# A three-deep store ring and W2 read in place by TensorE, in the expert stage of a graph-attention plus mixture-of-experts layer

## What is computed

```
x = x + elu(softmax(mask(leaky_relu(e), adj)) @ (layernorm(x) @ W))     # graph attention
n = layernorm(x)
idx = argmax(n @ router_w.T + router_b)                                 # one of 32 experts a token
h = relu(n @ W1[idx] + b1[idx])                                         # 256 -> 64
x = x + relu(h @ W2[idx] + b2[idx])                                     # 64 -> 256
```

## Time and profile before

| | |
|---|---|
| median of 3 runs | 1364.01 us (1361.14 to 1366.87) |
| the profiled execution's own time | 1360.98 us |
| its span (first to last instruction) | 1359.4 us |
| DVE busy over the span | 1064.8 us (78%) |
| PE / ACT / POOL busy | 827.6 / 729.6 / 619.2 us |
| the expert stage: first to last `yb` written | 1187.4 to 1346.6 us |

### The profile page before, as it was taken

How to read it: one execution, slowest core, us unless ns; L and a number is a source line. 1 busy time by engine, 2 the same in 40 slices (tenths; PEclk the granted TensorE clock), 3 DMA queues, 4 the chain that set the end, 5 groups by cost and what they waited for, 6 DMA issues and landing times.

```text
span 1359.4 us, 24132 instructions
## 1 busy us (share of the span) xinstructions
PE 827.6 (61%) x3116; PEld 631.0 (46%) x3116; DVE 1064.8 (78%) x4589; ACT 729.6 (54%) x1359; POOL 619.2 (46%) x651
## 2 busy tenths in 40 slices
PE   3766636666656656666665666566666775276663
PEld 2444435445444445445454454454544663154442
DVE  5888848888888888899988888889988764355553
ACT  3666846556666556665566655566654110155553
POOL 2111145544555445554455554545545772245553
PEclk9888956666666666666666666666666666589998
DMA  7999988887888887888888888878883246444442
GB/s 260 330 344 342 344 305 312 336 323 302 309 330 323 324 327 299 308 327 334 335 314 312 329 324 324 325 298 326 337 333 112 78 99 125 156 121 120 126 123 63
DMA packets 110969, 365.64 MB, mean 269 GB/s; under 512 B 28840, under 2 KB 62081, under 8 KB 78163
## 3 DMA queue, kind: packets, MB, share of 16 engines
q1 hardware_dynamic: 80610, 302.25, 59.5%
q0 software_dynamic: 28288, 61.66, 13.8%
q10 hardware_dynamic: 2034, 1.37, 0.3%
HBM read 352.05 MB, written 32.05 MB: 283 GB/s over the span
## 4 chain that ended last, share of the span: by engine, by line
DVE 40%; issue 28%; PE 12%; DMA 10%; DVEq 3%; POOL 3%; ACT 2%; POOLq 1%; ACTq 0%; SPq 0%
DVE top_word L854 7%; DMA out_x<-yb,tok 7%; DVE top_pos L860 4%; PE psL L1510 4%; DVE diag L1059 3%; PE psW L1431 2%; PE psT L1501 2%; PE psL L1511 2%; POOL G_all L590 2%; DVE xn L1103 2%; DVE st L909 1%; DVE el L1076 1%; DMA G_all<-wh_table,idx 1%; DVE begun L1002 1%; DVE code L868 1%
## 5 line engine op out<-in xcount | busy, mean ns | idle before, releaser
L590 POOL DMA_INDIRECT G_all<-wh_table,idx x384 | 399.0, 1039 | 231.5 <-issue 103.9
L699 ACT ACTIVATE sg<-raw_all,minus_half 128x2048 fp8e4<-128x2048 int32 x256 | 504.2, 1992 | 0.0
L1491 PE MATMUL psO<-G_all,diag 128*128 128x256 f32 x640 | 281.3, 623 | 91.8 <-DVE diag L1059 91.8
L1491 PEld LDWEIGHTS psO<-G_all,diag 128*128 128x128 f32 x640 | 200.7, 326 | 141.3 <-issue 96.4
L724 ACT ACTIVATE xT<-psT 128x256 f32<-128x256 f32 x64 | 24.5, 383 | 390.4 <-PE psT L1501 390.4
L854 DVE MAX8 top_word<-sg 128x8 f32<-128x512 f32 x256 | 174.4, 681 | 2.8 <-issue 0.4
L860 DVE FIND_INDEX8 top_pos<-top_word,sg 128x8 uint32<-128x512 f32 x256 | 175.3, 685 | 0.6 <-issue 0.6
L612 POOL DMA_INDIRECT regions<-x,posu x64 | 67.8, 1059 | 149.1 <-DVE posu L1141 145.9
L653 POOL DMA_INDIRECT out_x<-yb,tok x81 | 82.1, 1013 | 90.2 <-DVE yb L1376 72.0
L1431 PE MATMUL psW<-w_aug,xT 128*128 128x258 f32 x256 | 80.9, 445 | 8.0 <-ACT xT L691 7.6
L606 POOL TENSOR_TENSOR x<-ve,minus_half 128x1 f32<-128x1 f32 x64 | 36.0, 563 | 101.7 <-DVE x L1099 101.5
(11 more groups left out here) (209 smaller groups left out, 1882.9 us busy)
## 6 DMA issues: line engine op xcount, KB each, us to landing
raw_all<-in_adj SPq DMA_DIRECT2D x256, 1024.0 KB, 6.5
xb<-regions SPq DMA_DIRECT2D x84, 130.0 KB, 2.1
wh_table<-G_all POOLq DMA_DIRECT2D x8, 1040.0 KB, 11.0
w_sb<-in_x SPq DMA_DIRECT2D x8, 1024.0 KB, 8.2
xr<-in_x SPq DMA_DIRECT2D x64, 128.0 KB, 4.9
G_all<-wh_table,idx POOLq DMA_INDIRECT x384
w_sb<-in_L_ffn_W SPq DMA_DIRECT2D x2, 1024.0 KB
w_sb<-in_L_ffn_W SPq DMA_DIRECT2D x4, 512.0 KB
```

The lines of the kernel that those rows point to most:

```text
L590: pool.indirect_dma_start(out=G[par][:, k, :], out_offset=None, in_=table[:, :], in_offset=bass.IndirectOffsetOnAxis(ap=idx[par][:, k:k + ...
L699: act.activation(sg[par][q][:, :], raw[q], ACT.Sign, bias=minus_half[:, 0:1], saturate=False).then_inc(a_sg, 1)
L1491: pe.matmul(psO[par][:, 0:D], diag[:, k, :], G[par][:, k, 0:D], start=(k == 0), stop=False)
```

## The change

It has four parts in the expert stage and one at the start of the program.

- `yb`, `tok` and `y_out` come three times and not twice.
- DVE's `copy_w2` and the tiles `w2_b` are gone. PE's `block_output` reads the expert's number into a register and reads `w2_sb` in place at that offset. It has a wait on `v_y` (the rows of block b - 2 are written), which protects `psO`.
- b1 becomes a column of `w1_sb` behind the 128 columns of W1's two halves, 129 columns an expert. ACT makes one copy and not two. PE reads the stationary operand of half h at columns h*64 to h*64+128 of the copy.
- W1 is loaded by eight DMAs of half the size in place of four, b1 by one DMA that now stands behind the wait for the first stage's rows, and PE waits for the weights' arrival; DVE does not any more.
- Since the matmul reads 128 rows of `w2_sb`, rows 64 to 127 are set to zero by a DVE memset of 64 x 8192 elements among the program's first instructions. A plan instruction of DVE falls away.

```diff
+STORES = 3
-        w1_sb = sb("w1_sb", [P, E, DH, H])
-        b1_t = sb("b1_t", [H, E])
-        w2_sb = sb("w2_sb", [H + 1, E, D])
+        w1_sb = sb("w1_sb", [P, E, DH * H + 1])
+        w2_sb = sb("w2_sb", [P, E, D])
-        w1_b = [sb(f"w1_b{i}", [P, DH, P]) for i in range(2)]
-        b1_b = [sb(f"b1_b{i}", [H, 1]) for i in range(2)]
-        w2_b = [sb(f"w2_b{i}", [P, D]) for i in range(2)]
+        w1_b = [sb(f"w1_b{i}", [P, H + P]) for i in range(2)]
-        yb = [sb(f"yb{i}", [P, D]) for i in range(2)]
-        tok = [sb(f"tok{i}", [P, 1], u32) for i in range(2)]
+        yb = [sb(f"yb{i}", [P, D]) for i in range(STORES)]
+        tok = [sb(f"tok{i}", [P, 1], u32) for i in range(STORES)]
...
-                act.activation(b1_b[r % 2][:, :], b1_t[:, bass.ds(e, 1)], ACT.Copy)
-                act.activation(w1_b[r % 2][:, :, 0:H],
-                               w1_sb[:, bass.ds(e, 1), :, :].rearrange("p o h n -> p (o h) n"), ACT.Copy).then_inc(a_w1, 1)
+                act.activation(w1_b[r % 2][:, 0:DH * H + 1], w1_sb[:, bass.ds(e, 1), :].rearrange("p o n -> p (o n)"),
+                               ACT.Copy).then_inc(a_w1, 1)
...
-                v.memset(w1_b[par][:, :, :], 0.0)
-                v.memset(w2_b[par][:, :], 0.0)
+                v.memset(w1_b[par][:, :], 0.0)
+            v.memset(w1_sb[:, E - 1, DH * H:DH * H + 1], 0.0)
+            v.memset(w2_sb[H:P, :, :], 0.0).then_inc(w2_zero, 1)
             v.memset(slot_s[:, :], 0.0).then_inc(v_const, 1)
...
-                if not isinstance(b, int) or b > 1:
-                    v.wait_ge(y_out[r % 2], (b - r % 2) * 8)
+                if not isinstance(b, int) or b >= STORES:
+                    v.wait_ge(y_out[r % STORES], turn * 32 + r // STORES * 16)
...
-            blocks_loop(v, [(copy_w2, 2), (block_norm, 0), (block_rows, 3)])
+            blocks_loop(v, [(block_norm, 0), (block_rows, 3)])
...
+                e = pe.value_load(plan_i[0:1, bass.ds(b + P, 1)], min_val=0, max_val=E - 1)
                 pe.wait_ge(a_hT, b + 1)
-                pe.matmul(psO[r % 2][:, 0:D], hT[r % 2][:, :], w2_b[r % 2][:, :],
+                pe.wait_ge(v_y, b + RING - 1)
+                pe.nop(nofuse=True)
+                pe.matmul(psO[r % 2][:, 0:D], hT[r % 2][:, :], w2_sb[:, bass.ds(e, 1), :].rearrange("p o n -> p (o n)"),
                           start=True, stop=True).then_inc(pe_y, 1)
+            pe.wait_ge(ffn_in, 16 * 12)
```

More of the change, by code:

```diff
@@ L290, in gat_moe @@
         a_xb = sem("a_xb")
[L291 removed]
+        w2_zero = sem("w2_zero")
         a_w1 = sem("a_w1")
@@ L296, in gat_moe @@
         v_y = sem("v_y")
-        y_out = [sem(f"y_out{i}") for i in range(2)]
+        y_out = [sem(f"y_out{i}") for i in range(STORES)]
         VP = 8
@@ L653, in store_block @@
                 pool.indirect_dma_start(
[L654 to L656 removed]
+                    out=out[:, :], out_offset=bass.IndirectOffsetOnAxis(ap=tok[r % STORES][:, 0:1], axis=0),
+                    in_=yb[r % STORES][:, :], in_offset=None, bounds_check=last_row, oob_is_err=False
+                ).then_inc(y_out[r % STORES], 16)
             steps = blocks_loop(pool, [(store_block, TAIL)])
             with pool.If(steps > TURNS * RING):
[L660 to L663 removed]
+                for k in range(STORES):
+                    pool.wait_ge(y_out[k], 16 * ((BLOCKS + STORES - 1 - k) // STORES))
+                    pool.nop(nofuse=True)
             with pool.If(steps < TURNS * RING + 1):
[L665 to L667 removed]
+                rows_out = pool.value_load(steps_i[0:1, 1:2], min_val=16, max_val=16 * BLOCKS)
+                for k in range(STORES):
+                    pool.wait_ge(y_out[k], rows_out)
                     pool.nop(nofuse=True)
@@ L805, in hidden @@
                 act.wait_ge(a_w1, b + 1)
[L806 to L807 removed]
+                act.activation(hT[r % 2][0:H, :], psH[r % 2][0:H, 0:P], ACT.Relu,
+                               bias=w1_b[r % 2][0:H, DH * H:DH * H + 1]).then_inc(a_hT, 1)
+            act.wait_ge(ffn_in, 16 * 12)
             act.wait_ge(v_plan, PLAN_STEPS)
@@ L1372, in block_rows @@
                 v.wait_ge(pe_y, b + 1)
-                if not isinstance(b, int) or b > 1:
-                    v.wait_ge(y_out[r % 2], (b - r % 2) * 8)
-                v.tensor_copy(tok[r % 2][:, :], xb[r][:, D + 2:D + 3])
-                v.scalar_tensor_tensor(out=yb[r % 2][:, :], in0=psO[r % 2][:, 0:D], scalar=0.0, in1=xb[r][:, 0:D],
+                if not isinstance(b, int) or b >= STORES:
+                    v.wait_ge(y_out[r % STORES], turn * 32 + r // STORES * 16)
+                v.tensor_copy(tok[r % STORES][:, :], xb[r][:, D + 2:D + 3])
+                v.scalar_tensor_tensor(out=yb[r % STORES][:, :], in0=psO[r % 2][:, 0:D], scalar=0.0, in1=xb[r][:, 0:D],
                                        op0=ALU.max, op1=ALU.add).then_inc(v_y, 1)
-            def copy_w2(b, r, turn):
-                e = v.value_load(plan_i[0:1, bass.ds(b + P, 1)], min_val=0, max_val=E - 1)
-                v.tensor_copy(w2_b[r % 2][0:H + 1, :], w2_sb[:, bass.ds(e, 1), :].rearrange("p o n -> p (o n)")).then_inc(v_w2, 1)
-            v.wait_ge(ffn_in, 16 * 8)
-            blocks_loop(v, [(copy_w2, 2), (block_norm, 0), (block_rows, 3)])
+            blocks_loop(v, [(block_norm, 0), (block_rows, 3)])
         @block.tensor
@@ L1581, in block_hidden @@
                 for h in range(DH):
-                    mm = pe.matmul(psH[r % 2][:, 0:P], w1_b[r % 2][:, h, :], xTb[r % 2][:, h, :],
+                    mm = pe.matmul(psH[r % 2][:, 0:P], w1_b[r % 2][:, h * H:h * H + P], xTb[r % 2][:, h, :],
                                    start=(h == 0), stop=(h == DH - 1))
```

40 lines of the change are left out of this document (14 added, 26 removed).

## The result

| | changed | before, beside it |
|---|---|---|
| median | 1354.68 us (1348.75 to 1356.49, 6 runs) | 1363.87 us (1360.32 to 1366.87, 6 runs) |
| ratio | 0.9929 [0.9904, 0.9953] | |
| profiled execution: own time, span | 1356.24, 1354.6 us | 1360.98, 1359.4 us |
| first to last `yb` | 144.8 us, 1.81 a block | 159.2 us, 1.99 a block |

The kernel is 9.2 us faster; forecast were 31. The time lies outside the range of 1320 to 1350 us.

What follows compares the result with a forecast made beforehand. The two-buffer ring of stores was taken to bound the kernel at 1.99 us a block. The stage's -33.2 us and the start's +2.1 gave -31.1, so 1364.0 became 1333 us, range 1320 to 1350.

Steps and rivals of the forecast that it cites:

- The loads: Expert stage, refilling `xb`: landing plus some 0.35 us around it, 1.2 to 1.5 us a block, nearly always below other floors.
- The bulk: Expert stage after its first six blocks: 74 blocks at 1.54 us, from floors of 1.31 to 1.44 plus 0.1 for unevenness.
- the loop between DVE and PE: Expert stage: norm, transposes, `psO` and rows close a loop of two steps, 2.88 us, 1.44 a step, the highest floor.
- The six slow blocks: Start of the expert stage: at the 1.2 GHz clock level the first six blocks take 2.0 us each.
- The ring of stores: Expert stage, `yb` and `tok` stores: the 3.93 us round over three buffers becomes 1.31 us a block.
- PE's register load beside the array: PE's new load before `psO` runs beside transposes and hidden layer; first transpose to `psO` takes 1.2 us, 0.72 before.
- the rival of the stopped array: PE's register load waits for the matmuls ahead: 2.33 us a step, 1391 us in all; chance 7 in 100.
- POOL's floor: Expert stage, issuing stores: when ready, one starts 1.35 us after the one before, the least POOL needs a block.
- The clock: PE's granted clock in the expert stage: 0.99 before, and the denser steps should keep it there.
- The start: Start of the program: the longer memset row, 6.9 us, delays `w_t` from 8.82 to 10.9, costing 2.1 us.
- ACT: Expert stage: 1.49 us a step, 0.72 of it register load between `hT` and `b_b`; one copy fewer gives 1.38.
- What costs nothing: W1 in eight loads and PE's added wait on `v_y` were taken to add no time.

Runs made afterwards that it cites:

- e1_again: The changed kernel run again without any edit, in the first session: 1329.86 us, ratio 0.9745 to before.
- e7: Changed kernel with one more register load a block on SP, between the buffer wait and the DMA: 1382.05 us, ratio 1.0112.
- e8: Kernel before with one more register load a block on SP, between the buffer wait and the DMA: 1381.85 us, ratio 1.0107.
- e2: Kernel before with the third store buffer alone: 1331.88 us, ratio 0.9766.
- e11: Changed kernel without the runtime bounds check behind SP's register load: 1332.18 us, ratio 0.9792.
- e12: Changed kernel without bounds checks on SP's, PE's and ACT's register loads, without the memset, output matmul over 65 rows: 1318.67 us, ratio 0.9688.
- e3: Kernel before with the memset of 64 x 8192 elements alone: 1365.54 us, ratio 1.0014.
- e4: Changed kernel without the memset, its output matmul reading 65 rows: 1325.06 us, ratio 0.9722.
- e14: Kernel before, without any edit, profiled in a session where SP stalled: 1358.37 us, ratio 0.9983.

## Why the prediction was wrong

**The step that failed is "The loads".** It put "some 0.35 us around" the landing and took it from there that the loads' loop, 1.2 to 1.5 us a block, lies "below the others nearly always". With SP as in the profile of before this was right: in e1_again SP's delay is 0.35 us, at worst 0.79. In the record's profile it was 1.92 us, because SP's sequencer stalled, and it was not a longer loop but a lower rate: one load in 1.81 to 1.83 us. From the first to the last `yb` it made 144.8 us of the forecast's 126.0, and these 18.8 are most of what is missing: the profiled execution took 1356.2 us where 1329.9 were forecast for it, and the 26.3 us between them are these 18.8 and a first `yb` 8.2 us later than the 1189.5 us that the forecast gives, with 0.7 us won behind the last `yb`. The 8.2 us hold the start's error (below, 1.5 us) and, for the rest, differences of the first two stages that no run here takes apart. The prediction looked at SP only as part of a round trip and never asked how often it can issue. That question would have given SP's own floor, 1.12 to 1.17 us a block undisturbed, and some more at the turn's end: a fifth floor beside 1.44, 1.38, 1.35 and 1.31, and the one that rises first when its sequencer stalls. I had no row that showed the stalls, and no rival had them. Of the five times of this program two lie in the forecast's range (1329.9 and 1325.7 us) and three outside it, so the outcome on record depended on a condition that the forecast didn't know of.

Shown: the two times of the same program, 1325.7 to 1329.9 and 1354.0 to 1363.7 us, go with SP's long instructions in all five of its profiles (0 and 1 against 149, 161 and 199); the kernel before has both conditions without a difference in its stage (1.97 and 2.01 us a block); and work added to SP moves the time of both kernels (e7, e8). Not shown: what stalls SP. In the four sessions of experiments it was there on chips 1 and 3 and absent on chips 5 and 3, and all profiled kernels of a session had it or none; the pair on record differs in it (161 long instructions against 0), and whether its two profiles were taken under the same conditions isn't known. A load with a fixed address, which needs no register, and loads shared between SP and ACT were not tried.

The other steps, by the sessions in which SP is quick:

- **The bulk, 1.54 us a block**: the size is right, 1.52 over the last 74 steps of e1_again, but by luck in part. In the loop between DVE and PE, norm to transposes took 0.80 us on average in e1_again (0.46 was taken), transposes to `psO` 0.96 (1.2) and `psO` 0.69 (0.60). Together these are 2.45 us for 2.26, so the same loop comes to about 3.07 us, 1.53 a step and not 1.44, and the +0.1 for unevenness stood in for a term that was too small. This is my estimate from means; which part of PE's stream makes the norm wait longer was not tested. e2 fits the way the loop was drawn: with the load and copy of W2 on DVE, the prediction's 2.40 + 0.6 us and its +0.1 give 1.60 a block, and 1.61 were measured.
- **The six slow blocks**: too large. The first six steps of e1_again took 9.4 us for the 12.0, since the first `yb` is written when most of the low clock is over. The whole stage took 121.8 us for the 126.0, and the program 1329.9 for the 1333, with the start's error the other way. The two stretches before and behind it, in e1_again (us, busy by engine, granted clock, DMA share, GB/s), with the clock at 0.50, the 1.2 GHz level, as in the earlier trace rows, and then at 0.83, a mean over both levels:

```profile
1189.00:1198.00 9.00, 4.92 (x20) 4.24 (x21) 2.17 (x7) 2.79 (x9) 0.00 (x0) 0.50 0.36 90
1197.00:1203.00 6.00, 5.62 (x33) 4.68 (x32) 3.08 (x12) 3.73 (x12) 2.99 (x3) 0.83 0.40 110
```

- **The ring of stores, 1.31**: right that it leaves the first place. `tok` waits for stores 11 times and 5.8 us in e1_again; in e11 (17 times, 12.2 us) and e12 (30 times, 22.2 us) it is seen again.
- **PE's register load beside the array**: right, and the rival of the stopped array is dead. The `TENSOR_LOAD` takes 0.31 us as in the earlier trace rows (median 0.305, at worst 0.543), and the gap ahead of `psO` is small:

```profile
1240.98 0.26 PE psW L1570 x2
1241.25 0.45 PE psL L1578 x4
1241.69 0.20 issue
1241.90 0.69 PE psO L1589 x2
```

This is the chain of e1_again: from the first transpose to `psO` 0.92 us, where 1.2 was taken. Over 75 steps the gap between the hidden layer's last matmul and `psO` is 0.12 us on average and 0.51 at most. The weight load for `psO` waits for issue 53 times, 0.4 us each. The other figure, 600 ns, that the Trainium skill (DMA: Bandwidth & Descriptors, Latency and other measured facts) gives as a `tensor_load`'s floor would have meant 1344 us; the trace shows half of it on PE and on SP alike.

- **POOL's floor, 1.35**: a little lower. A store starts 1242.49 - 1241.22 = 1.27 us after the one before when both are ready, 0.08 below the 1.35 of the earlier trace rows. The two lines, from e1_again:

```profile
1241.22 0.97 POOL L655 DMA_INDIRECT out_x<-yb,tok  x1 [1.16 <-DVE yb L1376]
1242.49 0.97 POOL L655 DMA_INDIRECT out_x<-yb,tok  x1 [0.30 <-issue]
```

- **The clock** stayed up, as forecast, and also when PE waited for loads. The bulk of the stage, e1_again and then the record (us, busy by engine, granted clock, DMA share, GB/s):

```profile
1203.00:1319.00 116.00, 103.64 (x610) 78.69 (x610) 67.53 (x229) 75.16 (x230) 73.69 (x78) 1.00 0.55 158
```

```profile
1200.00:1340.00 140.00, 111.13 (x615) 78.03 (x613) 67.12 (x230) 75.97 (x230) 74.59 (x77) 1.00 0.45 133
```

As many instructions in 116 as in 140 us: DVE, ACT and POOL are busy equally long in both, and what was added is waiting.

- **The start, +2.1 us**: mis-sized, by a row that was read wrongly. The memset's row has the forecast length, 6.88 us for 6.9, but the engine also stands idle for 1.75 us ahead of it, in the changed kernel from 3.69 us on and in e3 from 4.37. The row that the forecast went by has the same: the earlier trace rows show 0.81 us of idle time ahead of `G_all`. From the end of the instruction before to the memset's own end, 4160 elements take 0.81 + 3.52 = 4.33 us, 1.04 ns each, and 8192 take 8.63 us, 1.05 each. The idle time grows with the length, so I count it to the memset; what VectorE does in it no trace shows. The one cycle per element that the Trainium skill (VectorE: DVE Perf Modes, Zero memsets can be issued as uint32) states, 8.5 us here, agrees with these times, and the prediction was wrong to set the row's length against it. `w_t` came 3.6 us later, where the row gave 2.1 and the skill's rule 3.7, and by e3 and e4 that costs the program between 2.3 and 4.8 us.
- **ACT**: the 0.72 us from `hT` to `b_b` are not all the register load, as the prediction reads them; half of it is `hT` itself, 0.36 us, and the idle time is 0.36. The floor of 1.38 us doesn't hang on it.
- **What costs nothing**: true of W1 in eight loads, for which no engine waits in the stage. The wait on `v_y` does end last now and then: in e1_again PE's `psO` waits for DVE's `yb` 11 times, 2.4 us in all, at most 0.4; in the record's profile it doesn't. What this costs the time was not tested.

## What to carry to other kernels

When a ring is made deeper, work out the next limit for every engine that takes part in a block, the one that only issues transfers among them: once as a round trip against the buffers, which more buffers can hide, and once as a rate, which they can't. The slack of the old kernel, here 2.2 us between a load's landing and its use, hides how an issuing engine behaves, so a short time in its profile is no promise. And before a result that contradicts a well-supported sum is explained, run both kernels again in another session and compare code that the change doesn't touch: here the second stage's `dma_start` told at once that something else than the changed lines was different, and the kernel before profiled with the stalls (e14) that the change isn't needed for it. And a row's length alone is not the price of an instruction: measure from the end of the one before it to its own end.

## What the runs showed of the hardware

- SP's sequencer can be in a condition in which single instructions, an 18 ns `SEQ_ASSERT` as well as a 333 ns `DMA_DIRECT2D`, take up to 0.72 us, some 150 to 200 times between 200 and 1100 us. Empty spaces of 0.65 to 0.76 us between two of its instructions come with it: 100 to 158 in that stretch in the eight profiles with 149 or more long instructions, none in the other nine. In that stretch none of DVE's, ACT's or POOL's sequencer instructions in the record's profile is over 0.4 us (DVE has 2 to 7 such in the second session); PE's weight-load queue has 58 such, but as many in e1_again.
- PE's sequencer loads a register while the array works off the matmuls ahead: 0.2 us of gap for a sequence whose register load alone takes 0.31.
- A memset of 64 x 8192 float32 elements has a row of 6.88 us, 0.84 ns an element, and 1.75 us of idle time ahead of it; one of 128 x 4160 has 3.52 and 0.81. Counted from the end of the instruction before, both take 1.04 to 1.05 ns an element.
- Indirect stores of 128 x 256 float32 elements that are ready follow one another 1.27 us from start to start on POOL, with 0.97 us busy each (e1_again).
